# Attention's x turned by VectorE in 32x32 blocks that pass through DRAM, instead of by TensorE

## The reference

```
h = layernorm(x) * (1 + ca) + sa
x = x + ga * linear_attention(h)       # 16 heads of 32, q and k through elu + 1.0001, causal, W_qkv and W_out 512 wide
h = layernorm(x) * (1 + cb) + sb
x = x + gb * ffn(h)                    # 1536 wide, silu(gate) * up, int32 weights times 1/127
```

## Time and profile before

| | us |
|---|---|
| median of 3 runs (lowest to highest) | 1996.96 (1995.05 to 2000.71) |
| profiled execution, its own time | 1998.45 |
| span of the profile, first to last instruction | 1996.7 |
| TensorE's mean granted clock | 0.998 |

### The profile page before, as it was taken

How to read it: one execution, slowest core, us unless ns; L and a number is a source line. 1 busy time by engine, 2 the same in 40 slices (tenths; PEclk the granted TensorE clock), 3 DMA queues, 4 the chain that set the end, 5 groups by cost and what they waited for, 6 DMA issues and landing times. The chain is left out here.

```text
span 1996.7 us, 43856 instructions
## 1 busy us (share of the span) xinstructions
PE 1960.6 (98%) x16008; PEld 1591.9 (80%) x16008; DVE 1443.1 (72%) x2386; ACT 905.7 (45%) x1542; POOL 877.4 (44%) x718
## 2 busy tenths in 40 slices
PE   7999999999999999999899999999999999999999
PEld 4788888888888888887678888788888888888887
DVE  7977888878788878787865857658576585765744
ACT  5443444344444434443344535445354453544533
POOL 2533544444544444453334443444434444344444
PEclk9999999999999999999999999999999999999999
DMA  7223333444434434432575654656546565465553
GB/s 268 69 91 102 115 123 119 135 130 133 135 100 133 128 125 135 127 110 90 179 263 176 207 187 145 214 170 209 186 144 215 171 210 186 144 214 174 169 168 106
DMA packets 202521, 309.81 MB, mean 155 GB/s; under 512 B 16145, under 2 KB 72977, under 8 KB 202386
## 3 DMA queue, kind: packets, MB, share of 16 engines
q1 hardware_dynamic: 201858, 306.78, 48.1%
q10 hardware_dynamic: 528, 1.05, 0.1%
HBM read 225.19 MB, written 82.58 MB: 154 GB/s over the span
## 5 line engine op out<-in xcount | busy, mean ns | idle before, releaser
L1497 POOL TENSOR_TENSOR h_lo<-y_rows,h_hi 128x512 fp32r<-128x512 f32 x192 | 246.5, 1301 | 367.6 <-ACT h_hi L1595 367.6
L461 POOL TENSOR_TENSOR x_res<-y,x_res 128x512 f32<-128x512 f32 x64 | 86.6, 1353 | 294.0 <-DVE y L872 283.5
L851 DVE TENSOR_TENSOR probs<-sc,causal 128x512 f32<-128x512 f32 x256 | 158.5, 681 | 3.8 <-PE sc L1156 2.6
L612 ACT ACTIVATE z_exp<-pj,qk_neg 128x512 f32<-128x512 f32 x128 | 87.7, 686 | 161.5 <-PE pj L1137 158.0
L1137 PE MATMUL pj<-xt_hi,w_hi 128*128 128x512 f32 x512 | 145.9, 406 | 5.7 <-DVE a_t L861 4.7
L1925 PE MATMUL sc<-wd,h_hi 128*128 128x512 f32 x384 | 150.7, 392 | 0.0
L1925 PE MATMUL sc<-wd,h_lo 128*128 128x512 f32 x384 | 149.6, 389 | 0.0
L450 POOL TENSOR_TENSOR a_lo<-a_t,a_hi 128x512 fp32r<-128x512 f32 x60 | 82.2, 1370 | 144.8 <-ACT a_hi L626 144.8
L1137 PE MATMUL pj<-xt_lo,w_hi 128*128 128x512 f32 x512 | 138.1, 391 | 1.8 <-DVE xt_lo L789 1.8
L1137 PE MATMUL pj<-xt_hi,w_lo 128*128 128x512 f32 x512 | 138.1, 392 | 0.0
L1710 DVE TENSOR_TENSOR r_den<-pj,k_tok 128x512 f32<-128x512 f32 x96 | 66.3, 691 | 97.9 <-ACT k_tok L1578 52.2
(11 more groups left out here) (248 smaller groups left out, 5390.4 us busy)
## 6 DMA issues: line engine op xcount, KB each, us to landing
w_hi<-parts SPq DMA_DIRECT2D x48, 1024.0 KB, 5.4
w_lo<-parts SPq DMA_DIRECT2D x48, 1024.0 KB, 5.4
x_mid<-x_res SPq DMA_DIRECT2D x96, 256.0 KB, 2.8
x_res<-in_L_attn_x SPq DMA_DIRECT2D x64, 256.0 KB, 2.8
k_dram<-k_block SPq DMA_DIRECT2D x252, 64.0 KB
xg<-in_L_attn_x SPq DMA_DIRECT2D x15, 1024.0 KB, 7.4
x_res<-x_mid SPq DMA_DIRECT2D x60, 256.0 KB, 3.9
full<-x_mid SPq DMA_DIRECT2D x60, 256.0 KB, 3.7
```

The lines of the kernel that those rows point to most:

```text
L461: pool.tensor_tensor(out=x_res[:, slot, :], in0=y[:, :], in1=x_res[:, slot, :], op=ALU.add).then_inc(y_ready, 1)
L612: act.activation(z_exp[:, n % 2, :], pj[:, n % 2, :], ACT.Relu, bias=qk_neg[:, 1 - kind, c:c + 1], scale=-scale).then_inc(below_ready, 1)
L851: dve.tensor_tensor(out=probs[:, h, :].rearrange("p (c i) -> p c i", c=C), in0=sc[:, h, :].rearrange("p (c i) -> p c i", c=C), in1=causal[ ...
L1497: pool.tensor_tensor(out=h_lo[b], in0=h[i], in1=h_hi[b].bitcast(F32), op=ALU.subtract).then_inc(h_lo_ready, 1)
```

## The change

For groups 2 to 15 the x of a group is no longer turned by PE. DVE norms x in place; ACT writes the normed group to a DRAM tensor `x_norm` (`save_x`, one DMA of 1 MB) and reads it back with four DMAs of 256 KB (`load_blocks`), each of which takes a quarter of the channels (128 of 512) of all 512 tokens into 32 partitions, in runs of 128 floats; DVE turns the 32x32 blocks of all of it in place with one transpose of 128x2048 (`turn_x`), and `xt_full` reads `xg` instead of a bank of PSUM. The channels come out in another order (`REGROUPED`), to which the host permutes the rows of W_qkv and of the modulation weights, and the first two groups' x (`x_first`).

The orders change with it. SP: `load_group` ahead of `load_units`, and waiting, since `xg` is read to the end by ACT, for `xf_ready` instead of `xt_ps`. DVE: all four `norm_stats` in tile 0 behind `v_rows`, `norm_var` behind the first `feature`, `norm_x` in tile 1 behind `mask`, `turn_x` in tile 2, the first two `xt_low` later by some instructions. POOL: `rstd_of` ahead of the first residual. ACT: `save_x` behind unit 2 (the third), `load_blocks` behind unit 4 (the fifth), `xt_full` behind unit 7. Group 0 has its own, later places. PE's `scores` wait for `xf_ready` in group 0 and in group 14 and later alone, and `x_turn` stays for the two groups written out first and for the first feed-forward group.

```diff
         def load_group(g):
-            wait(sp, xt_ps, C * g)
-            sp.dma_start(xg[:, :, :], x_groups[g, :, :, :] if isinstance(g, int) else
+            if isinstance(g, int) and g < 3:
+                wait(sp, xt_ps, C * g)
+            else:
+                wait(sp, xf_ready, C * g)
+            sp.dma_start(xg[:, :, :], x_first_groups[g, :, :, :] if isinstance(g, int) and g < 2 else
+                         x_groups[g, :, :, :] if isinstance(g, int) else
...
         def group(g, parity):
-            if not isinstance(g, int):
-                load_units(g, parity)
             if not isinstance(g, int) or g + 2 < NG:
                 load_group(g + 2)
+                if not isinstance(g, int):
+                    load_units(g, parity)
...
             last_bias(g, 0)
+            if two_ahead and not (isinstance(g, int) and g == 0):
+                rstd_of(g + 2)
...
-            act.activation(xf[:, c % 2, :], bank, ACT.Identity, bias=mod_col[:, SA, c:c + 1],
+            to, turned = xf[:, c % 2, :], bank
+            if not isinstance(g, int) or g >= 2:
+                to = to.rearrange("p (b i) -> p b i", i=E)
+                turned = xg[:, :, :].rearrange("p t (b c i) -> p c (t b) i", c=C, i=E)[:, c, :, :]
+            act.activation(to, turned, ACT.Identity, bias=mod_col[:, SA, c:c + 1],
                            scale=mod_col[:, CA, c:c + 1]).then_inc(xf_ready, 1)
+
+        def save_x(g):
+
+            wait(act, xn_ready, g + 1)
+            act.dma_start(x_norm.rearrange("(t p) d -> p t d", p=P), xg[:, :, :]).then_inc(x_saved, 16)
+
+        def load_blocks(g):
+
+            wait(act, x_saved, g * 16 + (-16))
+            for h in range(HPC):
+                act.dma_start(xg[h * E:(h + 1) * E, :, :].rearrange("p t (b x) -> p (t b) x", x=P),
+                             x_norm[:, h * P:(h + 1) * P].rearrange("(b i) x -> i b x", i=E)).then_inc(x_blocks_in, 16)
...
             exp_relu(n, 2)
+            if not g_last_turn and not at_start:
+                save_x(g + 2)
             exp_relu(n, 3)
             exp_relu(n, 4)
+            if not g_last_turn and not at_start:
+                load_blocks(g + 2)
             state_out(g * GT + 1)
...
             exp_relu(n, 5)
+            if at_start:
+                save_x(g + 2)
+                load_blocks(g + 2)
             exp_relu(n, 6)
-            xt_full(g + 2, 0, x_bank)
-            xt_high(g + 2, parity, 0)
...
             exp_relu(n, 7)
...
+            elif not at_start:
+                xt_full(g + 2, 0, x_bank)
+                xt_high(g + 2, parity, 0)
...
+        def turn_x(g):
+
+            wait(dve, x_blocks_in, g * (16 * HPC) + (-16 * HPC))
+            blocks = xg[:, :, :].rearrange("p t d -> p (t d)")
+            dve.transpose(blocks, blocks).then_inc(xt_ps, C)
...
             if not first:
                 v_rows(g, parity, 3)
+                norm_stats(g + 2)
...
             feature(n, other, 0)
+            if not first:
+                norm_var(g + 2)
             spread(g * GT, g, parity, 0)
             feature(n, other, 1)
             k_blocks(g, parity, 1)
             gate_last(g, 0)
-            if not first:
-                norm_stats(g + 2, range(3))
             divide(g * GT, g, parity, 0)
...
             mask(g * GT + 1)
-            norm_stats(g + 2, range(0 if first else 3, GT))
-            norm_var(g + 2)
+            if first:
+                norm_stats(g + 2)
+                norm_var(g + 2)
+            else:
+                norm_x(g + 2)
...
             feature(n, other, 4)
-            norm_x(g + 2)
+            if first:
+                norm_x(g + 2)
             divide(g * GT + 1, g, parity, 1)
...
             den_of(n, 1)
+            if turned and not first:
+                turn_x(g + 2)
             feature(n, other, 6)
-            xt_low(g + 2, parity, 0)
             feature(n, other, 7)
             gate_last(g, 2)
...
-            if not isinstance(g, int) or g + 2 <= NG:
+            if isinstance(g, int) and g == 0:
+                pe.wait_ge(xf_ready, 2 * C)
+            elif isinstance(g, int) and g + 2 == NG:
                 wait(pe, xf_ready, (g + 2) * C + (0, 0, 0, 2)[t])
...
-                if t >= 2:
+                if t >= 2 and isinstance(g, int) and g + 2 == NG:
                     wait(pe, probs_ready, (g * GT + t) * HPC + 4)
                     x_turn(g + 2, 2 * t - 4, x_bank)
...
-            if t >= 2 and ahead:
+            if t >= 2 and isinstance(g, int) and g + 2 == NG:
                 x_turn(g + 2, 2 * t - 3, x_bank)
...
+REGROUPED = np.arange(D).reshape(HPC, C, E).transpose(1, 0, 2).reshape(D)
```

More of the change, by code:

```diff
@@ L66, in groups, with build @@
         body(g, g % 2)
-def build(nc, x, w_qkv, b_qkv, b_cols, w_out, b_out, c_vec, c_row, w_mod, w_mod_t, ffn_words, out):
+def build(nc, x, x_first, w_qkv, b_qkv, b_cols, w_out, b_out, c_vec, c_row, w_mod, w_mod_t, ffn_words, out):
     top = ExitStack()
@@ L81, in build @@
         x_mid = nc.dram_tensor("x_mid", (L, D), F32, kind="Internal").ap()
+        x_norm = nc.dram_tensor("x_norm", (GN, D), F32, kind="Internal").ap()
         k_dram = nc.dram_tensor("k_dram", (P, D), F32, kind="Internal").ap()
@@ L185, in attention @@
 def attention(nc, s, sem, sbuf, psum, ident, gb_dram, mod_col, half_neg, w_hi, w_lo, xt_hi, xt_lo, ga_row,
-              gabo_row, bv_row, qk_bias, qk_neg, causal, den, den_eps, r_tok, c_col, norm, turned, later, wide, x, w_qkv, b_qkv,
-              b_cols, w_out, b_out, c_vec, c_row, w_mod, w_mod_t, ffn_words, x_mid, k_dram, parts, downs):
+              gabo_row, bv_row, qk_bias, qk_neg, causal, den, den_eps, r_tok, c_col, norm, turned, later, wide, x, x_first, w_qkv, b_qkv,
+              b_cols, w_out, b_out, c_vec, c_row, w_mod, w_mod_t, ffn_words, x_mid, x_norm, k_dram, parts, downs):
     WQ, WK, WV, WO = 0, D, 2 * D, 3 * D
-    xg, stats, mean_var, var_eps, rstd, x_in, ln_chain, var_ready, rstd_ready, xn_ready = norm
+    xg, stats, mean_var, var_eps, rstd, x_in, ln_chain, var_ready, rstd_ready, xn_ready, passed = norm
     z_exp = sbuf(s, "z_exp", [P, 2, GN])
@@ L211, in attention @@
     r_heads = r_den[0][:, 0, :]
-    init_done, dve_passed = sem("init_done"), sem("dve_passed")
+    init_done, dve_passed = sem("init_done"), passed
+    x_saved, x_blocks_in = sem("x_saved"), sem("x_blocks_in")
     xr_in, y_out = [sem(f"xr_in{i}") for i in range(2)], [sem(f"y_out{i}") for i in range(2)]
@@ L241, in attention @@
     x_groups = x.rearrange("a (g t p) d -> (a g) p t d", t=GT, p=P)
+    x_first_groups = x_first.rearrange("(g t p) d -> g p t d", t=GT, p=P)
     x_tiles = x.rearrange("a (t p) d -> (a t) p d", p=P)
@@ L402, in group @@
                     sp.wait_ge(y_out[slot], 16 * GT // 2 * (half + 1))
-                sp.wait_ge(xt_ps, C * (NG + half))
+                sp.wait_ge(*((xf_ready, C * NG), (xt_ps, C * (NG + 1)))[half])
                 sp.dma_start(xg[:, :, :], mid_groups[half, :, :, :]).then_inc(x_in, 16)
@@ L544, in group @@
             last_bias(g, 1)
-            if two_ahead or last:
+            if last or isinstance(g, int) and g == 0:
                 rstd_of(g + 2)
@@ L684, in ahead_of_last @@
             looped = not isinstance(g, int)
+            g_last_turn = not looped and g + 2 == NG
+            at_start = not looped and g == 0
             exp_relu(n, 0)
@@ L700, in ahead_of_last @@
             exp_relu(n, 5)
+            if at_start:
+                save_x(g + 2)
+                load_blocks(g + 2)
             exp_relu(n, 6)
-            xt_full(g + 2, 0, x_bank)
-            xt_high(g + 2, parity, 0)
+            if g_last_turn:
+                xt_full(g + 2, 0, x_bank)
             exp_relu(n, 7)
[L705 to L708, removed]
+            if g_last_turn:
+                xt_full(g + 2, 1, x_bank)
+            elif not at_start:
+                xt_full(g + 2, 0, x_bank)
+                xt_high(g + 2, parity, 0)
+                if looped:
+                    act.wait_ge(down_out, g * 16 + (-16))
+                xt_full(g + 2, 1, x_bank)
+                xt_high(g + 2, parity, 1)
             state_out(g * GT + 2)
@@ L712, in ahead_of_last @@
                 unit_to_float(g, parity, 1)
+            if at_start:
+                for c in range(2):
+                    xt_full(g + 2, c, x_bank)
+                    xt_high(g + 2, parity, c)
             xt_full(g + 2, 2, x_bank)
@@ L973, in ahead_of_last @@
             first = isinstance(g, int) and g == 0
+            turned = looped or g + 2 < NG
             mask(g * GT)
@@ L1016, in ahead_of_last @@
             den_of(n, 2)
-            xt_low(g + 2, parity, 1)
             if looped:
                 word_size(g, 2, r_den[other][:, 3, :], (unit_in[1], g * 16 + (-16)))
+            if not first:
+                xt_low(g + 2, parity, 0)
             mask(g * GT + 3)
             v_rows(n, other, 0)
+            if first:
+                turn_x(g + 2)
```

(19 more changed lines are left out.)

13 lines of the change are left out of this document (7 added, 6 removed).

## The result

The changed kernel takes **2032.33 us** (median of 4 runs, 2031.42 to 2034.31) against 1996.72 for the kernel before beside it: ratio 1.0177, 95% interval 1.0162 to 1.0192, 35.6 us slower. Forecast were 2013 us, 16 us slower. The profiled execution took 2034.31 us with a span of 2032.6, where before had 1996.7.

What follows compares the result with a forecast made beforehand. PE, busy 98% of the span, was taken as the bound. 7 (loop) + 2.5 + 2.5 - 1.2 (groups outside) + 5 (clock) = +16 us: 2014.4 for the profiled execution, 2013 us as median, range 1992 to 2034.

Steps and rivals of the forecast that it cites:

- 3.1 us a group: Looped groups: PE stands still ahead of tile 1's scores, from T+14.15 to gate_last's end at T+17.3, against 2.51 saved.
- not every one need do it; I take three falls, 5 us: Clock behind the new waits at tile 1's scores: three falls to 0.50, 5 us in all.
- rival 1: The clock falls in every looped group: 20 us instead of 5, giving 2028 us; chance 0.14.
- T+7.2: Landing of x, counted from T, the start of tile 0's scores; taken between T+6.4 and T+9.8.
- nothing large is ahead of it: SP's load of x, now ahead of the words: reason for taking group 1's row, landed 5.6 us after issue.
- 10.1 were worked out: DVE in tile 0, from x's landing at T+7.2 to gate_last's end at T+17.3.
- Group 0's +2.5: Group 0: ACT waits for the write between units 5 and 6; about 4 us of waiting less 1.88.
- Group 1's -1.2: Group 1, no words: x at T+6.8, a wait of 1.3 against 2.5 saved.
- Group 14's +2.5: Group 14 keeps its x_turns but has the new DVE order: about 3.1 - 0.6.
- Rival 2: Blocks read back from DRAM come late, turn_x over 2 us late, tile 3's scores wait: 20 us more, 2033; chance 0.10.
- Rival 4: Faster: DVE's free time ahead of the first feature takes in the norm_stats; x at T+5.5 gives about 1985; chance 0.14.
- T+6.6: Rival 4's deciding point for x's landing, where the wait at tile 1's scores equals the 2.5 saved.

Runs made afterwards that it cites:

- the order alone: Kernel before, transposes still on PE, with only the changed places of x's load, norm_stats, norm_var, norm_x and rstd: 2035.26 us, ratio 1.019.
- without the pass: Changed kernel without save_x and load_blocks, turn_x turning the normed x where it lies, so computing something else: 2029.77 us, ratio 1.0161.
- the early load: Changed kernel with SP issuing the load of x ahead of the store and load of k that end the group before: 1982.82 us, ratio 0.9925.
- the clock kept up: Changed kernel with ten matmuls whose result nobody reads ahead of tile 1's scores in each looped group: 2014.92 us, ratio 1.0088.
- the one with the words ahead of x: Changed kernel with norm_stats and norm_var behind tile 0's divide and the words issued ahead of x again: 1990.18 us, ratio 0.9965.
- the two runs with norm_stats behind the divide: Changed kernel with norm_stats and norm_var behind tile 0's divide: 2016.9 us; the same with words issued ahead of x: 1990.18 us.
- the first with better places: Early load of x plus norm_var, den_of of unit 1, group 0's load_blocks and group 14's norm_stats moved later: 1993.17 us, ratio 0.9975.

## Why the prediction was right or wrong

**Right: the place, the mechanism and the sign.** PE was said to be 0.58 us from waiting at tile 1's scores, and to stand there for 3.1 us a group on a gate that hangs on the landing of x. It stands 3.45 us on average. What PE saves came as worked out: tile 3 -0.95 of 0.94, tile 2 -1.42 of 1.57 (in five groups tile 3's scores wait for 0.11 to 0.50 us, inside the 0 to 0.5 given).

**The step that failed: "not every one need do it; I take three falls, 5 us".** The clock falls behind 11 of the 12 standstills in the loop; the one that it spares is the shortest, 2.03 us in group 3. Eight falls last 3.41 us and three 6.83, and tile 1 is 1.73 us longer on average, 20.8 us in 12 groups where 5 were set down. This was rival 1, at a chance of 0.14, with a price of 20 us, and it is most of what came on top of the forecast. The argument against it was that the wait is "only a little longer" than the one that the trace showed falling. That speaks for it: behind a wait longer than one with a fall a fall is to be expected, unless a row shows one without. The trace of before has a shorter one, 1.58 us ahead of tile 1 in group 14, behind which the tile takes 14.16 us; 3.1 lay beyond both. The Trainium skill, "TensorE: Matmul & The Clock Gate", section "HAM oscillation — how this bites in real kernels", whose kernel waits once in every step and begins every step at the low clock, was the better guide: here its picture holds in 11 groups of 12.

**Smaller: when x lands.** T+7.2 was taken, T+8.62 measured. Of the 1.42 us 0.53 is the issue, T+2.13 for 1.6: that the last gate of a group comes nearer to the next T without the x_turns was said and not added (the order alone, with the x_turns, has T+1.59, nearly the number taken). The rest, 0.89, is the transfer, 6.5 us for 5.6: group 1's row has no words behind it, and "nothing large is ahead of it" is not the same as nothing beside it. Group 1 of the changed kernel, still without words, took 5.6 again. The line of that load, looped groups, issue to landing:

```profile
DMA to landing us min/median/max: 5.4/6.5/7.3
```

Against that the way from x's landing to the gate's end is 9.03 us, where 10.1 were worked out: var_eps takes 0.17 us (L814 above) where the earlier trace rows had 0.99. In the kernel before POOL works on a residual during each of the 12, in the changed kernel on nothing. The two make 1.42 - 1.07 = 0.35 us more wait a group, 4 us in all; that 3.1 us came so near to the 3.45 measured is luck in part, since the two errors all but cancel.

**Smaller: outside the loop.** Group 0's +2.5 came as +2.2, though at other places: PE waits 2.35 us for ACT ahead of the numerators in tile 2 and 1.35 us for DVE's v_rows in tile 3. Group 1's -1.2 came as -0.7. Group 14's +2.5 came as +0.1: its wait is 2.42 us without a fall of the clock, and the kernel before already waited 1.58 there, a row that I had not looked at.

**Rival 2, late blocks, fell.** turn_x never waited for its blocks, and without the pass the time is 2.6 us less. But that the two extra megabytes a group cost "nothing" was wrong: they make the load of k later, and DVE waits 0.81 us a group for it ahead of turn_x. Here little of that reaches PE. In the faster orders the wait (1.3 us a group with the early load) stands in DVE's queue ahead of the gate of tile 3's scores; what it costs there no run shows. The line of turn_x (ns shortest, median, longest):

```profile
L828 DVE STREAM_TRANSPOSE xg<-xg x14: 2267/2270/2302, 117.9 to 910.9; 128x2048 f32<-128x2048 f32 x14
```

The write of 1 MB (L617), issue to landing:

```profile
DMA to landing us min/median/max: 4.3/4.4/6.0
```

The four reads of a group (L623), each, issue to landing:

```profile
DMA to landing us min/median/max: 3.2/5.3/7.7
```

The turn was taken at 2.4 us and the write at 5.6. The warning of "DMA: Bandwidth & Descriptors", section "Anatomy of one DMA — SWDGE (gpsimd) path", of the Trainium skill, that the signal of a write to HBM can be long delayed, did not bite here, where ACT issues the write: 4.4 us for 1 MB.

**Rival 4's case came about another way.** It said that the change pays with x at T+6.6 or sooner, and asked for a faster transfer; the early load brought x to T+3.4 to T+6.0 by a sooner issue, and the time to 1982.8 us, where the rival had 1985 for x at T+5.5. The nearness is luck in part: the loop gave 16.9 us where the rival had 13.2, the groups outside cost 3.1 where it had 1. T+6.6 itself was too strict: group 3 of the changed kernel had x at T+7.15, kept its clock and took 58.62 us, 0.42 less than before. On average the change as made was not near that point.

## What to carry to other kernels

Work that is put ahead of the instruction that hands a bank back to the bottleneck engine costs its input's arrival, not its own duration: ask first when the input lands, and what lands behind it. If the engine has free time there and only the input is late, move the load and not the work. And a standstill of TensorE that repeats is to be priced with the clock that follows it, at each repetition, once the trace has a fall behind a wait no longer than it.

## What the runs showed of the hardware

The granted clock behind a standstill isn't decided by its length alone. From PE's timelines of the kernel before, of the change and of six of the experiments (left out are the clock kept up and the one with the words ahead of x), the standstill ahead of tile 1's scores in groups 1 to 14, from 0.18 us on, and how long tile 1 then took, in number of tiles:

```
standstill, us      tile 1 at 14.12 to 14.16    at 15.61 to 17.02
0.18 to 1.74         24                          0
1.78 to 3.08         9                          18
3.13 to 4.62         0                          19
```

(One tile of 15.31 us behind 0.68 is not counted; it has another wait in it.) The first row is no bound. Ahead of tile 3's scores the clock fell seven times behind 1.61 to 2.47 us, in the two runs with norm_stats behind the divide and in the first with better places, while other waits there of up to 2.25 us left it at full speed. Each fall ahead of tile 1 costs 1.5 to 2.9 us beside the standstill itself. What decides in the middle row stays open; the lengths of low clock seen in the loop of the changed kernel were 3.41 and 6.83 us and none between.

A load's time went with what was queued around it: the same 1 MB of x took a median of 7.8 us in the loop of the kernel before, with the words ahead of it, 6.5 in the change with the words behind it, and 8.1 with the words ahead of it again. The load of k took a median of 4.2 us in the change and 3.1 with the pass through DRAM left out.
